# Context attentions of a decoder: K/V projections in one piece behind the scores, four places for copied scores, reciprocals moved behind the clamp or between the maxima

## What is computed

```python
# layer 0: 16 heads of 16, biases, scores clamped
attn = einsum('bhqd,bhkd->bhqk', q, k) * scale
attn = softmax(clip(attn, -CLAMP, CLAMP), axis=-1)
x = x + einsum('bhqk,bhkd->bqhd', attn, v).reshape(B, Nq, Cq) @ Wo + bo
# layer 1: 8 heads of 64
attn = softmax(einsum('bhid,bhjd->bhij', q, k) * scale, axis=-1)
x = x + (attn @ v heads side by side) @ Wo + bo
# layer 2: 16 heads of 16, masked
scores = where(context_mask[:, None, None, :], scores, max_neg)
x = x + (softmax(scores) @ v heads side by side) @ Wo
```

## Time and profile before

| | us |
|---|---|
| median of three runs | 3099.77 |
| profiled execution, its time | 3105.24 |
| its span (first to last instruction) | 3103.5 |
| PE busy | 2613.3 (84%) |
| DVE busy | 1446.2 (47%) |
| ACT busy | 1289.6 (42%) |
| POOL busy | 890.6 (29%) |

### The profile page before, as it was taken

One profiled execution on the slowest core, in us unless ns is written; L12 is line 12 of the kernel. 1 busy time (PEld: TensorE's weight loads), 2 busy tenths in 40 slices (PEclk: granted clock), 3 DMA queues, 4 the chain that ended last, 5 costly groups with the idle time before them and its releaser, 6 DMA issues. The chain is left out here.

```text
span 3103.5 us, 56465 instructions
## 1 busy us (share of the span) xinstructions
PE 2613.3 (84%) x18499; PEld 1924.0 (62%) x18500; DVE 1446.2 (47%) x3474; ACT 1289.6 (42%) x3858; POOL 890.6 (29%) x572
## 2 busy tenths in 40 slices
PE   5746899879777988998599877999959996989899
PEld 2345666656455555666489734666649995866566
DVE  5685888850544234444522376566550004654211
ACT  1334677742443123333223222677724342862211
POOL 3254455520001022222133244455522222430000
PEclk8867899979898999999899987999979998989899
DMA  2000000000142010000357600000045553013100
GB/s 104 1 1 27 20 16 20 15 30 1 40 107 66 0 44 16 20 15 15 124 192 238 211 33 33 21 20 19 11 186 186 180 184 100 1 43 89 40 14 24
DMA packets 108484, 194.45 MB, mean 63 GB/s; under 512 B 56276, under 2 KB 81060, under 8 KB 96596
## 3 DMA queue, kind: packets, MB, share of 16 engines
q1 hardware_dynamic: 93986, 166.93, 16.8%
q0 software_dynamic: 6816, 18.62, 2.0%
q10 hardware_dynamic: 7570, 7.47, 0.8%
HBM read 174.29 MB, written 18.71 MB: 62 GB/s over the span
## 5 line engine op out<-in xcount | busy, mean ns | idle before, releaser
L1353 POOL TENSOR_TENSOR L_xattn_p<-L_xattn_p,L_xattn_ri 112x1500 f32<-112x1500 f32 (+1 forms) x192 | 435.9, 2270 | 586.6 <-DVE L_xattn_ri L1661 586.6
L1566 ACT ACTIVATE L_xattn_pT<-ps 125x448 f32<-125x448 f32 (+1 forms) x576 | 255.8, 478 | 356.7 <-PE ps L1457 356.5
L1457 PEld LDWEIGHTS ps<-ident,L_xattn_p 112*125 112x125 f32 x1920 | 256.0, 191 | 100.5 <-issue 40.5
L1578 ACT ACTIVATE L_xattn_p<-L_xattn_sa,L_xattn_ng 112x375 f32<-112x375 f32 x512 | 305.1, 603 | 18.1 <-DVE L_xattn_ng L1677 10.4
L1457 PE MATMUL ps<-ident,L_xattn_p 112*125 112x112 f32 x1920 | 292.2, 284 | 9.5 <-POOL L_xattn_p L1353 4.9
L1009 PEld LDWEIGHTS ps<-L_ffn_xsT,L_ffn_w 128*128 128x128 f32 x2240 | 263.7, 194 | 7.0 <-issue 1.9
L1009 PE MATMUL ps<-L_ffn_xsT,L_ffn_w 128*128 128x128 f32 x2240 | 264.7, 277 | 2.4 <-ACT L_ffn_xsT L1039 2.4
L276 POOL TENSOR_TENSOR ln_rstd<-ln_tmp,half 112x8 f32<-112x8 f32 x26 | 44.3, 1719 | 701.2 <-DVE ln_tmp L225 525.1
L1479 PE MATMUL ps<-L_xattn_kT,L_xattn_qm 32*112 32x375 f32 (+1 forms) x1280 | 173.3, 523 | 70.1 <-DVE L_xattn_v L1604 21.4
L1071 DVE TENSOR_TENSOR L_ffn_y<-ps,L_ffn_pack 128x256 f32<-128x256 f32 x70 | 29.7, 425 | 364.6 <-PE ps L1018 364.6
L1018 PE MATMUL ps<-L_ffn_weights,L_ffn_hT 128*128 x840 | 193.5, 380 | 2.3 <-DVE L_ffn_hT L1083 2.3
(11 more groups left out here) (410 smaller groups left out, 5083.4 us busy)
## 6 DMA issues: line engine op xcount, KB each, us to landing
L_ffn_w<-in_L_ffn_experts SPq DMA_DIRECT2D x74, 1024.0 KB, 5.5
L_xattn_src<-in_ctx SPq DMA_DIRECT2D x48, 375.0 KB, 3.0
L_attn_toeplitz<-L_attn_h SPq DMA_DIRECT2D x4, 3136.0 KB, 23.1
L_ffn_weights<-in_L_ffn_experts SPq DMA_DIRECT2D x8, 1028.0 KB, 16.8
L_xattn_keys<-in_ctx SPq DMA_DIRECT2D x16, 281.2 KB, 6.0
L_xattn_rows<-in_ctx_rows SPq DMA_DIRECT2D x16, 281.2 KB
L_ffn_weights<-in_L_ffn_experts SPq DMA_DIRECT2D x8, 516.0 KB, 9.5
L_ffn_w<-in_L_ffn_experts SPq DMA_DIRECT2D x4, 1026.0 KB, 5.9
```

The source lines that it names most:

```text
L1353: g.tensor_tensor(P[:, m % 4, :, :], P[:, m % 4, :, :], ri[:, m % 4, :].unsqueeze(2).broadcast_to([T, W, S2]), ALU.mult).then_inc(s["prob_ ...
L1457: last = pe.transpose(turned(t)[:, j * T:(j + 1) * T], P[:, m % 4, j, kc * KW:(kc + 1) * KW], k.ident[0:T, 0:T])
L1566: act.activation(PT[:, m % 4, kc, :, :].rearrange("p h t -> p (h t)"), turned(t), ACT.Copy).then_inc(s["pt_ev_a"].sem, 1)
L1578: last = act.activation(P[:, m % 4, j, :], at, ACT.Exp, bias=ng[:, m % 4, j:j + 1], scale=-1.0 if mask else 1.0, accum_out=rs[:, m % 4, j: ...
```

## The change

It does three things.

1. PE, layer 1 (W = 2): `close_pair` stands directly behind `open_pair`, ahead of `weigh` and `turn_over`. With W = 4 PE's order stays.
2. Layers 0 and 2: `sa` has four places and not two, so DVE's write for step n waits for the exponentials of unit n-4 and not of unit n-2. In layer 2 this wait is carried by a new small copy of one column, `pace`, ahead of the maxima.
3. DVE's order. Layer 0: `share` stands behind the clamp, and the second half of the maxima behind the store of a V or K job (steps 0 and 1). Layer 2: `share` stands between the two halves of the maxima, and so at step 2 also behind the early V store. Layer 1's DVE order stays.

```diff
--- before.py
+++ after.py
@@ -1226,7 +1226,8 @@
     V = sb("v", [KW, 2, KN, HD // R, R + (E - 1) * dh])
     qm = sb("qm", [KP, 2, E, C, T])
     bqs = sb("bqs", [KP, E * C])
-    sa = sb("sa", [T, 2, W, S2]) if copied else None
+    sa = sb("sa", [T, 4, W, S2]) if copied else None
+    pace = sb("pace", [T, 1]) if mask else None
     P = sb("p", [T, 4, W, S2])
     PT = sb("pT", [KW, 4, KN, W, T])
     oT = sb("oT", [KP, 2, C, T])
@@ -1507,14 +1508,14 @@
                 score(i, n)
                 if W == 2:
                     open_pair(i, n)
+                    close_pair(i, n)
                 weigh(i, n - OUT, first, b)
                 if W == 4 and early:
                     open_pair(i, n)
                     close_pair(i, n)
                 turn_over(i, n - TURN, (0, 1), first)
-                if W == 4 and not early:
+                if not early:
                     open_pair(i, n)
-                if W == 2 or not early:
                     close_pair(i, n)
                 ask(i, n)
                 answer(i, n, first)
@@ -1574,7 +1575,7 @@
                         act.wait_ge(*s["pt_mm"].at((i * U + m - 3) * KN))
                     act.wait_ge(*s["max_done"].at((i * U + m) * HALVES + h + 1))
                     for j in range(2 * h, 2 * h + 2):
-                        at = sa[:, m % 2, j, :] if copied else scores(m)[:, j, :]
+                        at = sa[:, m % 4, j, :] if copied else scores(m)[:, j, :]
                         last = act.activation(P[:, m % 4, j, :], at, ACT.Exp, bias=ng[:, m % 4, j:j + 1],
                                               scale=-1.0 if mask else 1.0, accum_out=rs[:, m % 4, j:j + 1])
                     if h == HALVES - 1:
@@ -1666,12 +1667,12 @@
                     return
                 b, u, p = batch_of(i, n)
                 r = n % 4
-                at = sa[:, n % 2, :, :] if clamp else scores(n)
+                at = sa[:, n % 4, :, :] if clamp else scores(n)
                 for h in halves:
                     two = slice(2 * h, 2 * h + 2)
                     if mask:
                         for j in range(2 * h, 2 * h + 2):
-                            last = v.tensor_tensor_reduce(sa[:, n % 2, j, :], at[:, j, :], mb[:, u, :], -1.0, FMAX,
+                            last = v.tensor_tensor_reduce(sa[:, n % 4, j, :], at[:, j, :], mb[:, u, :], -1.0, FMAX,
                                                           ALU.add, ALU.min, ng[:, r, j:j + 1])
                     else:
                         last = v.tensor_reduce(ng[:, r, two], at[:, two, :], AX.X, ALU.max, negate=True)
@@ -1680,25 +1681,33 @@
             def step(i, n, first, last_turn):
                 b, u, p = batch_of(i, n)
                 early = W == 4 and p == jobs[J_V2][3]
-                if not mask:
-                    share(i, n - 1 - LATE, first)
+                if not copied:
+                    share(i, n - 1, first)
                 if n < U:
                     if mask and p == 0:
                         v.wait_ge(*s["mask_done"].at(b + 1))
                     v.wait_ge(*s["sc_mm"].at(i * U + n + 1))
                     if clamp:
-                        v.wait_ge(*s["exp_done"].at(i * U + n - 1))
-                        v.tensor_scalar(sa[:, n % 2, :, :], scores(n), CLAMP, -CLAMP, ALU.min, ALU.max).then_inc(
+                        v.wait_ge(*s["exp_done"].at(i * U + n - 3))
+                        v.tensor_scalar(sa[:, n % 4, :, :], scores(n), CLAMP, -CLAMP, ALU.min, ALU.max).then_inc(
                             s["sc_read"].sem, 1)
-                if mask:
-                    share(i, n - 1 - LATE, first)
+                    elif mask:
+                        v.wait_ge(*s["exp_done"].at(i * U + n - 3))
+                        v.tensor_copy(pace[:, :], k.half[:, 0:1])
+                if clamp:
+                    share(i, n - 2, first)
                 if early:
                     keep(i, n, "KV")
                 if clamp and n < U:
                     v.wait_ge(*s["sc_read"].at(i * U + n + 1))
-                maxima(i, n, range(HALVES))
+                maxima(i, n, (0,))
+                if mask:
+                    share(i, n - 2, first)
+                    maxima(i, n, (1,))
                 if not early:
                     keep(i, n, "KV")
+                if clamp:
+                    maxima(i, n, (1,))
                 keep(i, n, "Q")
                 add(i, n, first)
                 if mask and p == UB // 2 and not (last_turn and n >= UB):
```

## The result

| | median us (lowest to highest) | runs |
|---|---|---|
| before | 3100.49 (3097.92 to 3105.62) | 6 |
| after | 3089.62 (3088.12 to 3091.31) | 6 |

The ratio is 0.9963, with a 95% interval of 0.995 to 0.9976: the change saves 10.9 us, 0.37%. I had forecast 3076, 24 us less. The direction is right and the size is not; the range (3061 to 3091) holds the time, at its very end. A second set of the same kernel gave 3092.23 beside 3103.72, a ratio of 0.9966 (0.9955 to 0.9977).

What follows compares the result with a forecast made beforehand. PE was the fullest engine in all three layers, so its remaining waits set the time. Terms -15 - 12.5 + 4.5 = -23 took the profiled 3105.2 to 3082, 3076 from the runs' median; range 3061 to 3091.

Steps and rivals of the forecast that it cites:

- Layer 0, -15: Layer 0: both PE waits, for the K store and the clamp, go; 1.0 us a batch, 15 batches, -15 us.
- The chain: Layer 0: scores of step 3 through DVE's clamps, reciprocal, POOL's multiplication and PE back to those scores, 19.74 against 20.74 us.
- The rival by which PE's floor is reached (18.8): Layer 0: reciprocals are never late, batch falls to 18.8 us, -29 in place of -15, total 3062; 12%.
- Layer 1, -12.5: Layer 1: earlier stores save 2.17 us a batch, new waits cost 2 x 0.67; batch 21.87, -12.5 us in 15.
- The old waits: Layer 1: PE's waits for the V store, 1.28 us, and a K store, 0.89, go: -2.17 a batch.
- the two new ones: Layer 1, steps 0 and 2: third transposes wait for ACT's emptying, +0.41 us; next job's first piece for exponentials, +0.26.
- The rival of this layer (the waits eat the gain): Layer 1: exponentials behind late transposes cost 2.17 us a batch, total 3089; 12%.
- Layer 2, +4.5: Layer 2: PE's 0.79 us wait goes, a 1.11 delay comes; +0.3 a batch, +4.5 us in 15.
- The term for the wait: Layer 2: step 2's late reciprocal delays POOL, so PE's transposes start 1.11 us later.
- `pace` at nothing: Layer 2: the one-column copy, bounded between nothing and 0.18 us, costs nothing, as DVE has air.
- The rival of the lock: Layer 2: `pace` and step 2's mask copy wait for POOL's multiplication, some 0.2 us a batch, total 3079; 5%.
- Outside the stages, 0: Outside the three layer stretches: no time changes, since the layer parts are blocks that follow one another.

Runs made afterwards that it cites:

- l1_only: The kernel before with only layer 1's part, both pieces of a K or V job directly behind the scores: 3096.83 us, 0.9977 of before.
- l1_turn_first: The changed kernel with the first two parts of layer 1's transposes ahead of `weigh`: 3064.41 us, 0.9881 of the kernel before.
- l2_share_ahead: The changed kernel with layer 2's reciprocal of step 2 ahead of the early V store again: 3071.71 us, 0.99 of the kernel before.

## Why the prediction was right and wrong

- **Layer 0, -15: right in mechanism, a little small.** The chain gave 19.74, measured 19.58; all its links are there, and PE's new wait is for POOL ahead of the transposes of step 1, as it said. I had not seen that it waits at step 0 too. 1.16 x 15 = 17.4; the first batches give 3 more (22.52 and 22.35 before, 20.71 and 19.08 after, from one scores of step 0 to the next), where I had counted on steady batches alone. 1.6 of these 3 are luck, as they hang on the clock of one execution: in `l1_only`, with layer 0 as before, the second of them took 20.74, at a granted clock of 1.00 and not 0.92. The rival by which PE's floor is reached (18.8) fell.
- **Layer 1, -12.5: the term that was mis-sized; it measured -4.5.** Of 0.83 us a batch 0.29 came. The old waits went as forecast, the two new ones came at the places named and with about the size given (third transposes 0.91 us behind the first ones' start, forecast 0.93; the job's piece 0.96 behind the scores, forecast 0.98). The step that failed is the one never written down: that PE's own 20.53 us stay the same when its instructions are put in another order. The batch came out 0.54 over my 21.87. About 0.2 of that is the order, as `l1_turn_first` shows, which has no wait left and takes 20.75; in the rows it goes with one late load more at steps 0 and 2. The other 0.3 comes with the four waits, whose loads begin late too. The rival of this layer (the waits eat the gain) was nearer to the truth than the forecast, by another mechanism than it gave.
- **Layer 2, +4.5: right to 0.03 us in the batch.** The term for the wait was 1.11 and is 1.03. `l2_share_ahead` shows it: with the reciprocal ahead of the V store the loss turns into a gain of 13 us in the stage. The stage as a whole cost 7.4 and not 4.5, mostly since its first batches ran at a lower clock.
- **`pace` at nothing: right.** It takes 0.15 us with DVE idle ahead of it. The rival of the lock was half right. The row with the mask's copy shows it held for most of POOL's multiplication, 1.43 us and not 0.35; `pace` is not held where it runs inside a multiplication (DVE, then POOL):

```profile
2078.46 0.15 DVE L1696 COPY L_xattn_pace<-half 112x1 f32<-112x1 f32 x1 [0.27 <-PE ps L1480]
```

```profile
2076.31 2.69 POOL L1354 TENSOR_TENSOR L_xattn_p<-L_xattn_p,L_xattn_ri 112x1500 f32<-112x1500 f32 x1 [1.37 <-DVE L_xattn_ri L1662]
```

The Trainium skill (SBUF — State Buffer, on the two sides of SBUF) says that a VectorE op in a two-port mode and a GpSimd op exclude each other. The trace agrees for the mask's 375 columns. `pace` was not excluded, so what failed is my reading that a copy of one column is such an op too; no run here shows from what size it would be. The total of 3079 that this rival gave had the right cause at one of its two places, but the copy's wait costs PE nothing here: the scores of step 0 at 2097.45 have no bracket.
- **Outside the stages, 0: wrong.** The sum of my terms, mended, is -17.4 - 4.4 + 4.5 = -17. Measured are -11. Between kernels with the same instructions behind layer 2 that part moves by up to 6.6 us, and a delay alone moves it by 3.5 to 4.2, and layer 2's stage by about 4. That is as large as the terms of the sum, and my range had nothing for it.

So of the 13 us by which the forecast missed, 8 are layer 1's term, 2.4 go the other way in layer 0's batches, and the rest, some 7, lies outside steady batches. It is a balance: 3 in layer 2's first batches, 3.1 behind layer 2, and the 4.7 by which the profiled execution of before was over its median, less 3 in layer 0's first batches and 0.7 elsewhere. For 2.3 of the first and 1.4 of the second the rows show a lower granted clock. The 4.7 may be what `l1_only` lacks in parts that it shares with before, 2.6 in layer 0 and 3.2 behind layer 2; that isn't shown, since the one trace of before is of that execution.

## What to carry to other kernels

When instructions are put in another order on a full engine, their own time isn't constant (here 0.2 us a batch, and 0.08 for each new wait): look at which weight loads begin ahead of their product. When a small instruction is moved behind others "where there is air", check every step of the pattern, since it is late only in the one step whose neighbours have another order; here one reciprocal in four, at step 2, cost 20 us. And before small differences outside an edit are explained, delay the same kernel by a few microseconds: if a 3 us delay costs 11 in one version and 3 in another, a difference of a few microseconds in untouched parts proves nothing of the edit.

## What the runs showed of the hardware

- An operation on DVE within SBUF that makes 375 float32 columns out of bytes took 1.43 us beside a POOL multiplication and ended 0.21 behind it, 0.35 alone; a copy of one column took 0.15 either way.
- PE's third transposes to scores took 0.40 us where their load began together with the product, behind a wait or directly behind `weigh`, and 0.30 where it began ahead. A 128-row product behind a 64-row one had such a late load and took 1.98 us, 1.89 otherwise.
- The unchanged parts behind layer 2 took 823.5 us, and 827.0 when they began some 8 us later behind a delay; in another kernel 829.8, and 825.6 when delayed. The granted clock at the start of its cross attention went between 1.00 and 0.88 in both. What in the moment of the start decides it is not settled by these runs.
